# A graph network's gathers: a wait for each tile's products instead of one for each unit

## The reference

```python
hsrc = h[src]                                   # layer 0: relational
for b in range(8):
    msg = msg + hsrc @ weight[b] * w_comp[etype][:, b][:, None]
node_repr = segment_sum(msg * norm, dst) + bias_param
x = layernorm(x + relu(node_repr))

neigh = segment_sum(x[src] + edge_feat, dst)    # layer 1: GIN
h = ((1 + eps) * x + neigh) @ W1 + b1
h = relu(batchnorm(h, gamma, beta)) @ W2 + b2
x = layernorm(x + h)
```

## Time and profile before

| | |
|---|---|
| median of 3 runs | 781.75 us |
| profiled execution | 781.48 us |
| its span, first to last instruction | 779.7 us |
| TensorE busy | 585.2 us |
| VectorE busy | 493.7 us |
| GpSimd busy | 418.9 us |
| ScalarE busy | 297.0 us |
| mean granted TensorE clock | 0.83 |

### The profile page before, as it was taken

One profiled execution on the slowest core, in us unless ns is written; L12 is line 12 of the kernel. 1 busy time (PEld: TensorE's weight loads), 2 busy tenths in 40 slices (PEclk: granted clock), 3 DMA queues, 4 the chain that ended last, 5 costly groups with the idle time before them and its releaser, 6 DMA issues.

```text
span 779.7 us, 13302 instructions
## 1 busy us (share of the span) xinstructions
PE 585.2 (75%) x3971; PEld 480.7 (62%) x3971; DVE 493.7 (63%) x1866; ACT 297.0 (38%) x672; POOL 418.9 (54%) x434
## 2 busy tenths in 40 slices
PE   4137877777878686888678877797787876999994
PEld 2025766655667574776556766666676665878764
DVE  7039666667569676777764887767774344536456
ACT  9502444544455444445443544345340000000074
POOL 6730767667667665766765666666656666100000
PEclk9998657677875788757889788999889888999998
DMA  4400335455454654545744647566565562463002
GB/s 115 108 25 2 99 117 147 119 158 149 133 145 119 189 170 149 163 131 161 217 134 126 203 136 221 167 200 200 153 199 161 181 203 71 126 240 129 2 1 83
DMA packets 97035, 108.21 MB, mean 139 GB/s; under 512 B 10805, under 2 KB 81446, under 8 KB 96962
## 3 DMA queue, kind: packets, MB, share of 16 engines
q1 hardware_dynamic: 80898, 79.25, 32.6%
q0 software_dynamic: 13312, 27.29, 12.8%
q10 hardware_dynamic: 2752, 0.79, 0.4%
HBM read 81.73 MB, written 25.56 MB: 138 GB/s over the span
## 4 chain that ended last, share of the span: by engine, by line
DVE 34%; PE 34%; another core or an unknown queue 12%; issue 10%; DVEq 4%; ACT 3%; DMA 1%; ACTq 0%; SPq 0%
PE psum L1053 11%; DVE etype_hot L1388 7%; PE psum L999 6%; DVE etype_hot L1385 5%; PE psum L1029 5%; PE psum L1005 5%; DVE sums_flat L1509 5%; PE psum L1020 3%; DVE adj_flat L1479 3%; DVE weighted L1307 3%; DVE adj_flat L1283 2%; DVEq L1482 1%; ACT adj_flat L804 1%; DVE sums_flat L1463 1%
## 5 line engine op out<-in xcount | busy, mean ns | idle before, releaser
L716 POOL DMA_INDIRECT gathered_flat<-in_x_dram,src_i x416 | 416.6, 1001 | 247.3 <-issue 106.2
L999 PE MATMUL psum<-weighted,gathered_flat 128*128 128x160 f32 (+1 forms) x832 | 178.0, 342 | 23.4 <-issue 21.0
L999 PEld LDWEIGHTS psum<-weighted,gathered_flat 128*128 128x128 f32 x832 | 156.6, 238 | 42.1 <-issue 39.7
L1509 DVE TENSOR_TENSOR sums_flat<-psum,sums_flat 128x180 f32 x208 | 71.9, 346 | 168.8 <-remote 90.8
L1020 PE MATMUL psum<-etype_hot 128*128 128x300 f16 (+2 forms) x624 | 119.2, 313 | 48.4 <-issue 26.2
L778 ACT ACTIVATE adj_flat<-zero_col 128x450 f16<-128x450 f32 x208 | 108.4, 579 | 107.9 <-DMA adjacency<-adj_flat 66.6
L1005 PEld LDWEIGHTS psum<-hot,attrs 128*128 128x128 f32 x832 | 136.5, 231 | 9.5 <-issue 9.4
L1005 PE MATMUL psum<-hot,attrs 128*128 128x20 f32 (+1 forms) x832 | 131.0, 273 | 7.7 <-issue 7.7
L1388 DVE TENSOR_SCALAR etype_hot<-iota_key,key_t 128x300 f16<-128x300 f16 (+1 forms) x416 | 131.9, 318 | 0.0
L1020 PEld LDWEIGHTS psum<-etype_hot 128*128 128x128 f16 x624 | 69.7, 132 | 68.9 <-issue 43.0
L1385 DVE TENSOR_SCALAR etype_hot<-iota_key,gathered_flat 128x128 f16<-128x128 f16 x416 | 108.8, 262 | 0.1
(11 more groups left out here) (144 smaller groups left out, 345.6 us busy)
## 6 DMA issues: line engine op xcount, KB each, us to landing
attrs<-in_edge_attr_dram SPq DMA_DIRECT2D x51, 512.0 KB
adjacency<-adj_flat SPq DMA_DIRECT2D x26, 900.0 KB
sums_flat<-adjacency SPq DMA_DIRECT2D x13, 576.0 KB
gathered_flat<-in_x_dram,src_i POOLq DMA_INDIRECT x416
coef<-adjacency SPq DMA_DIRECT2D x23, 288.0 KB
sums_flat<-adjacency SPq DMA_DIRECT2D x5, 648.0 KB, 8.8
sums_flat<-adjacency SPq DMA_DIRECT2D x9, 288.0 KB
out_dram<-gathered_flat SPq DMA_DIRECT2D x6, 256.0 KB
```

The lines of the kernel that those rows point to most:

```text
L716: pool.indirect_dma_start(gathered[:, t % (RING * GROUP), :], None, x[:, :], bass.IndirectOffsetOnAxis(src_i[:, t:t + 1], 0)).then_inc(gat ...
L999: nc.tensor.matmul(ps[:, 0:B, STARTS[i]:STARTS[i] + WIDTHS[i]], gathered[:, (u * UNIT + i) % (RING * GROUP), 0:F], weighted_tiles(s, i)[:, ...
L1509: nc.vector.tensor_tensor(window, unit_psum(u), window, ALU.add).then_inc(added, 1)
```

## The change

A new semaphore `tiles_read` is raised by each product with gathered rows. GpSimd waits before the gather of tile t for t - 32 + 1 of them, instead of waiting before each unit for the couples counted by `sums_mm`. `sums_mm` stays for VectorE and SyncE.

```diff
+        tiles_read = sem("tiles_read")
...
             def gather_unit(u):
 
-                if u >= RU:
-                    pool.wait_ge(sums_mm, (u - RU) // 2 + 1)
                 for t in range(u * UNIT, (u + 1) * UNIT):
+                    if u >= RU:
+                        pool.wait_ge(tiles_read, t - RU * UNIT + 1)
                     pool.indirect_dma_start(
                         gathered[:, t % (RING * GROUP), :], None, x[:, :],
                         bass.IndirectOffsetOnAxis(src_i[:, t:t + 1], 0)).then_inc(gather_in[u % RU], 16)
...
                                          weighted_tiles(s, i)[:, u % GU, :, :],
-                                         start=(i == 0), stop=(i == UNIT - 1))
+                                         start=(i == 0), stop=(i == UNIT - 1)).then_inc(tiles_read, 1)
```

## The result

The changed kernel took 774.06 us (median of 16 runs, 769.42 to 779.98), the kernel before beside it on the same chip 782.63 us (16 runs, 779.2 to 788.72). The ratio is 0.989, with a 95% interval of 0.987 to 0.991. The prediction was no change, 781.6 us.

The account below looks back on a forecast made before the run. TensorE and VectorE handing work to each other were taken to set the time, with GpSimd beside the chain. Terms 0 + 0 + 0 + 0 left the forecast at 781.6 us, no change; range 777 to 787 us.

Parts of the forecast that it names:

- The waits on GpSimd: GpSimd's queue: 192 waits become 384; at most 1.9 us of its queue, cost on the path 0.
- The signals: TensorE: 416 matmuls now raise a semaphore; taken as 0, bounds -4.2 to +4.2 us.
- The transfers: DMA: gathers keep number and size, times move by up to 6 us; 3.4 us either way, taken as 0.
- rival B: Gathers collide with the counts' stores that ScalarE waits for; 5 us slower, 786.5 us; chance 0.09.
- When the gathers go: GpSimd's gathers start 0 to 6 us earlier, where 26 us of distance to TensorE are unused; gain 0.
- Rival C: Spreading gathers takes away a quarter of TensorE's 21.0 us idle before L999; 5.3 us faster, 776 us; chance 0.12.

Follow-up runs that it names:

- the increments alone: Kernel before plus 416 increments of tiles_read that nobody waits for; ratio 1.0008 and 1.0007 in quick sessions, 1.002 (776.63 against 775.68 us) in a slow one.
- one-a-couple kernel: Kernel before, but gathers wait for one tiles_read increment a couple, from its last product with x; 772.9 against 774.29 us, 0.9979, in a slow session.
- Runs of sixteen: Kernel before, but gathers come free sixteen at a time; 943.7 against 775.68 us, 1.2182, in a slow session; 1.024 and 1.0227 in quick ones.

## Why the prediction was wrong

- *The waits on GpSimd: 0.* Right. The idle time before the gathers is 247.3 us in both kernels, and the waits are named after the product with x, more and shorter, as forecast.
- *The signals: 0.* Right; the increments alone give 1.0008, 1.0007 and 1.002. The Trainium skill's 26.3 ns an increment ("TensorE: Matmul & The Clock Gate", section "The cost: per-tile semaphore tail") would have made 10.9 us by my estimate; the largest interval, up to 1.0041 of 776 us, leaves room for 3.2 us. The tiles of that section are parts of the matmul array in which small products run side by side, not this kernel's tiles of edges, and its figure is for a tail behind them; no run here shows that case.
- *The transfers: 0.* The sign was unknown, and nothing here speaks against it. ScalarE waits for its stores 72.2 us in 21 pieces, 5.6 us more than in the earlier trace rows, about rival B's price, but the trace is 7.1 us shorter: the wait moved and didn't decide the time. With the changed kernel repeated it was 61.9 us against 75.1 us of the kernel before in that session, so the move isn't even steady.
- *When the gathers go: "Gain: 0".* This is the step that failed. Its count was right: GpSimd is 31 tiles ahead where it was 28, and nothing waits for a gather (the landing for which it had no row and took 8.8 us is 2.4 us). What it put at 0 is a loop shorter by 7.1 us. What the step took for granted is that a gather touches TensorE only by what it brings. In the slow sessions it also does by how closely it follows others: eight in a row, and TensorE's own stream comes in pieces.

Rival C had the mechanism by its name ("if that bunching starves TensorE, spreading it takes some away") and the time (776 us), at a chance of 0.12. It placed the bunching at the start of a couple, where gathers, load and adds begin together; the pieces lie at the end of the run, after the seventh gather. The prediction had also said that a move of more than 4 us in TensorE's idle time before the counts' products means B or C: without a releaser it went from 26.2 to 35.5 us. I put it down with "nothing ties the gaps to that moment". That was true of the moment I looked at and of no other. The row that should have stopped me stood in my own list: a single record with 0.46 us before it inside a run, at 134.47 us. I used it as a sign that the stream "is not rigid", and did not set the other 30 beside GpSimd's timeline. The preparation between 29 and 47 us, where 2.6 us stand before a record with nothing to wait for, would have shown the same without any counting; I didn't look ahead of the loop since the change doesn't touch it.

That rival C named it is partly luck: its reason pointed at another moment, and its price was a quarter of the idle time before L999, while the real sum is 27 us fewer idle pieces, 42 us more waits and 20 us less busy time.

What is open. Which resource the gathers take from TensorE isn't shown. The fetching of instructions, as far as the profile has it, doesn't look slower: the page's queue q8 (kind "instruction", 34 packets of 16 KB) keeps step with TensorE's records (its eleventh packet comes after 1283 to 1320 of them in all 20 traces), and its packets take 1.1 us in the median in a slow session as in a quick one; none of them falls between 0 and 53 us in the kernel before, while the single records stand at 30 to 41 us. Whether it is the issuing of the gathers or their transfers that disturbs isn't separated either, since no run moved one without the other. Neither is shown what makes a session slow or quick: the durations of instructions on the other engines agree, and what differs is how closely TensorE's records follow each other. Whether recording has a part in it can't be told: every timed run here has a granted clock and a span on record too. And the one-a-couple kernel (0.9979) has 43 pieces of 21.5 us with more long runs than the kernel before, not fewer; by the length of runs alone it should be no better. With the pieces at the fourth gather and the changed kernel's waits at gathers 5 to 7, that says that length is not the whole rule.

## What to carry to other kernels

Idle time on an engine between instructions that wait for nothing ("issue") is a reading, not noise: list the pieces with their times, and set them beside every other engine's timeline, DMA issue above all, before you say that an engine off the chain costs nothing. Where GpSimd has slack, try it with indirect gathers in short runs (here mostly two to six) rather than as soon as it can. Pauses while GpSimd was well ahead cost nothing here and were worth 2.3% in slow sessions; where it has no slack, later gathers cost 1.2% to 2.4% (quick sessions). And run a small effect in more than one session: in the quick ones nothing that shortened the runs won more than 0.2%.

## What the runs showed of the hardware

- In slow sessions, TensorE's stream breaks into single records about 0.7 us or a multiple apart, mostly from the seventh or eighth back-to-back indirect gather on (128 rows, 1.25 us each; 29.5 of 36.0 us), seldom at or behind the fourth, and up to 2.8 us apart in a run of 32. From the twelfth gather of a run on TensorE started 0.9 records a us in place of 6.1. Runs of sixteen cost 22%.
- The same kernel takes 667 us in quick sessions. The busy time of VectorE, ScalarE and GpSimd is the same there to 1%, the loop has no idle piece inside a unit in place of 72, and its granted clock is 0.85 against 0.80 (trace of the kernel with the increments alone).
- In slow sessions TensorE also answers signals late: 5 to 14 waits a trace end over 0.5 us after the signal, none in a quick session.
- A gather of 128 rows of 512 bytes lands 2.4 us after its start in the median, 6.5 us at most (kernel before).
- An increment on a matmul in the middle of a run of products costs nothing that 416 of them would show: at most 3.2 us together, 8 ns each.
